# Two of chunk 1's tiles get their output projection inside the last group's steps, the other six tiles form one pipeline, and the FFN takes chunk 1 first

## The reference

```python
x = x + _L0_attn_ref(_layernorm(x), Wq, bq, Wk, bk, Wv, bv, Wo, bo)   # o @ Wo + bo
x = x + _L0_ffn_ref(_layernorm(x), ...)    # (silu(x Wg) * (x Wu)) Wd, 704 hidden, int weights
x = x + _L1_attn_ref(_layernorm(x), Wq, Wk, Wv, Wo)
x = x + _L1_ffn_ref(_layernorm(x), ...)    # 768 hidden, float8 weights with scales
```

## Time and profile before

| what | value |
|---|---|
| time, median of 3 runs | 446.37 us (446.0 to 446.38) |
| the profiled execution: time, span | 448.61 us, 446.9 us |
| PE busy | 414.6 us (93%) |
| DVE, ACT, POOL busy | 300.9, 235.1, 161.0 us |
| output projection, layer 0: first "on" to first FFN matmul | 165.05 to 180.77 us |
| the same, layer 1 | 388.37 to 405.89 us |

### The profile page before, as it was taken

One profiled execution on the slowest core, in us unless ns is written; L12 is line 12 of the kernel. 1 busy time (PEld: TensorE's weight loads), 2 busy tenths in 40 slices (PEclk: granted clock), 3 DMA queues, 4 the chain that ended last, 5 costly groups with the idle time before them and its releaser, 6 DMA issues.

```text
span 446.9 us, 14541 instructions
## 1 busy us (share of the span) xinstructions
PE 414.6 (93%) x6328; PEld 237.3 (53%) x6328; DVE 300.9 (67%) x608; ACT 235.1 (53%) x381; POOL 161.0 (36%) x242
## 2 busy tenths in 40 slices
PE   5799989999999979999999998998999999797997
PEld 5356654455555338444476465644545553384476
DVE  4635699999997118421335568899999971188883
ACT  3635545677677872311101552465776778725950
POOL 4118323202202232296881000235362553321780
PEclk9989999999999999999999998899999999999999
DMA  6799550000000000201000476400000000000002
GB/s 201 119 249 277 108 146 4 4 3 4 4 3 4 4 7 1 72 1 67 5 0 0 129 201 180 133 4 4 4 2 4 4 5 2 2 1 0 2 23 72
DMA packets 21657, 22.97 MB, mean 51 GB/s; under 512 B 2588, under 2 KB 20858, under 8 KB 21594
## 3 DMA queue, kind: packets, MB, share of 16 engines
q1 hardware_dynamic: 20498, 19.03, 17.0%
q0 software_dynamic: 544, 2.49, 1.8%
q10 hardware_dynamic: 552, 0.53, 0.4%
HBM read 8.27 MB, written 1.05 MB: 21 GB/s over the span
## 4 chain that ended last, share of the span: by engine, by line
PE 69%; DVE 17%; ACT 5%; DMA 3%; issue 3%; SPq 2%; POOL 1%; ACTq 0%; DVEq 0%
PE ps L701 11%; PE ps L721 11%; DVE mx L1110 11%; PE ps L679 10%; PE ps L803 8%; PE ps L868 5%; PE ps L808 5%; ACT prob L997 4%; PE ps L825 4%; PE ps L836 4%; PE ps L616 3%; DMA col_rows<-in_L_ffn_up_scale 3%; PE ps L687 2%; DVE stats L1074 1%; DVE xn L1183 1%
## 5 line engine op out<-in xcount | busy, mean ns | idle before, releaser
L1110 DVE TENSOR_REDUCE mx<-ps 128x1 f32<-128x512 f32 (+3 forms) x304 | 182.1, 654 | 25.7 <-PE ps L687 23.1
L997 ACT ACTIVATE prob<-ps 128x1024 f32<-128x1024 f32 (+1 forms) x192 | 145.5, 812 | 70.4 <-PE ps L701 69.8
L679 PE MATMUL ps<-kS,qS 99*32 99x512 bf16 (+18 forms) x1536 | 114.2, 322 | 5.1 <-DVE mx L1110 2.7
L530 POOL TENSOR_SCALAR_AFFINE_SELECT prob<-prob 128x256 f32<-128x256 f32 x128 | 51.9, 412 | 161.0 <-ACT prob L997 159.7
L701 PE MATMUL ps<-qS,kS 101*32 101x512 bf16 (+7 forms) x1536 | 96.6, 329 | 4.0 <-ACT prob L997 3.7
L721 PE MATMUL ps<-prob,v 128*32 128x512 f32 (+3 forms) x768 | 80.1, 489 | 2.1 <-POOL prob L530 1.4
L679 PEld LDWEIGHTS ps<-kS,qS 99*32 99x32 bf16 (+1 forms) x1536 | 43.8, 96 | 53.1 <-DVE mx L1110 29.1
L701 PEld LDWEIGHTS ps<-qS,kS 101*32 101x32 bf16 (+1 forms) x1536 | 35.3, 96 | 32.6 <-ACT prob L997 16.8
L684 PE MATMUL ps<-mask_q,identb 128*32 128x32 bf16 (+1 forms) x1024 | 52.2, 186 | 0.0
L687 PE MATMUL ps<-mask_q,identb 128*32 128x64 bf16 (+1 forms) x512 | 45.9, 198 | 0.0
L803 PE MATMUL ps<-xnT,gu0T 128*128 128x512 f32 x80 | 34.8, 594 | 0.7 <-ACT xnT L907 0.7
(11 more groups left out here) (141 smaller groups left out, 551.0 us busy)
## 6 DMA issues: line engine op xcount, KB each, us to landing
qS<-parts SPq DMA_DIRECT2D x24, 128.0 KB, 3.1
kS<-parts SPq DMA_DIRECT2D x24, 128.0 KB, 3.0
qS<-prob SPq DMA_DIRECT2D x12, 128.0 KB, 7.1
kS<-prob SPq DMA_DIRECT2D x12, 128.0 KB, 6.6
qS<-xn SPq DMA_DIRECT2D x12, 128.0 KB
kS<-xn SPq DMA_DIRECT2D x12, 128.0 KB, 2.6
out<-x SPq DMA_DIRECT2D x8, 128.0 KB, 1.7
oT<-in_L_ffn_gate_w POOLq DMA_DIRECT2D x1, 768.0 KB
```

The source lines that it names most:

```text
L530: nc.gpsimd.affine_select(out=square, in_=square, compare_op=ALU.is_ge, fill=0.0, base=0, pattern=[[0, 2], [1, P]], channel_multiplier=-1) ...
L679: mmi = nc.tensor.matmul(span[r:r + STRIP, 0:seen], qS[0:K_MAX[L], c, g * G + h, qt * P + r:qt * P + r + STRIP], kS[0:K_MAX[L], g * G + h, ...
L997: nc.scalar.activation(prob[:, n % 3, 2 * pair:2 * pair + 2, off:CH], ps[:, 2 * (m % 2):2 * (m % 2) + 2, off:CH], ACT.Exp, scale=SCALE).th ...
L1110: ins = nc.vector.tensor_reduce(mx[:, slot, qt, heads[0]:heads[-1] + 1, part], src, AX_X, ALU.max)
```

## The change

Chunk 1's tiles 4 and 5 (`EARLY`) get their three jobs inside the last pair's steps. `E_STEPS` places them: (1, 1) means step s1, behind its second scores; place 2 is behind the product with `v`. They use banks 4 to 6, with semaphores of their own, `e_full` (PE) and `e_free` (DVE). For them DVE, not ACT, copies `onT`.

The six other tiles form one pipeline in the order `RING`. At its last iteration with an "on" job, PE also transposes chunk 1's four normalised tiles. POOL, not DVE, normalises these (`xn_pool`). The FFN takes chunk 1 first; chunk 0's transposes stand behind 2 (layer 0) or 3 (layer 1) hidden tiles (`TURNS_BEHIND`), and DVE normalises chunk 0 behind its first FFN product. ACT's Silu table is loaded behind the ring's first `onT` copy. `FIRST_HALF_AFTER` becomes 6, with layer 0's "down" in the order 4, 5, 0, 1, 2, 3, 6, 7.

```diff
+FFN_C = (1, 0)
+TURNS_BEHIND = (2, 3)
+DOWN_ORDER = ((4, 5, 0, 1, 2, 3, 6, 7), (4, 5, 6, 7, 0, 1, 2, 3))
+LN_PAIRS = ((0, 1, 2, 3), (2, 3, 0, 1), (2, 0, 1, 3), (2, 3, 0, 1))
+EARLY = (4, 5)
+RING = (6, 7, 0, 1, 2, 3)
+E_STEPS = {(1, 1): [("on", 4)], (2, 0): [("turn", 4)], (2, 1): [("on", 5)], (2, 2): [("wo", 4)],
+           (3, 0): [("turn", 5)], (3, 2): [("wo", 5)]}
-FIRST_HALF_AFTER = 5
+FIRST_HALF_AFTER = 6
...
+                    if n // 2 % 2 and first >= TPC:
+                        pool.wait_ge(rstd_done, pair + 1)
+                        for t in (first, first + 1):
+                            nc.gpsimd.tensor_scalar(xn[:, t], x[:, t], mv[:, t, 0:1], rstd[:, t:t + 1],
+                                                    ALU.subtract, ALU.mult).then_inc(xn_pool, 1)
...
+            def early_job(L, kind, t):
+                bank = ps[:, e_bank(L, kind)]
+                if t > TPC:
+                    e_left(pe, L, kind, t - 1)
+                if kind == "on":
+                    if t == TPC:
+                        pe.wait_ge(m_free, (L + 1) * N_MAX)
+                        pe.wait_ge(o_taken, (L + 1) * N_CG - 1)
+                    mmi = query_major(bank, t)
+                elif kind == "turn":
+                    e_left(pe, L, "on", t)
+                    mmi = dim_major(bank, t)
+                else:
+                    e_left(pe, L, "turn", t)
+                    mmi = times_wo(L, bank, t)
+                mmi.then_inc(e_full, 1)
...
+                    if n == len(RING) - 1:
+                        ln_transposes("ffnT", 2 * L + 1, FFN_C[0], L, *((take_a, a_full) if L == 0 else (take_b, b_full)))
...
+                for kind, t in E_JOBS:
+                    dve.wait_ge(e_full, e_made(L, kind, t))
+                    bank = ps[:, e_bank(L, kind)]
+                    if kind == "on":
+                        divide(bank, t).then_inc(e_free, 1)
+                    elif kind == "turn":
+                        nc.vector.tensor_copy(onT[:, t % 2].rearrange("p j q -> p (j q)"), bank[:, 0:C]).then_inc(e_free, 1)
+                    else:
+                        nc.vector.tensor_tensor(x[:, t], bank[:, 0:C], x[:, t], ALU.add).then_inc(e_free, 1)
+                        e_left(dve, L, kind, t)
+                        ln_stats(t)
```

More of the change, by code:

```diff
@@ L205, in pace, with early @@
         return int(here)
+    last = len(exp_steps()) - TPC
+    def early(s, place):
+        order.extend(("early",) + job for job in E_STEPS.get((s - last, place), []))
     at = 0.0
@@ L215, in attention_order @@
             order.append(("pv", s - PV_LAG))
+        early(s, 2)
         at += wide(s)
@@ L535, in rstd_of @@
                 for pair in range(2 * n, 2 * n + 2):
-                    tiles = slice(2 * (pair % 4), 2 * (pair % 4) + 2)
+                    first = 2 * LN_PAIRS[n // 2][pair % 4]
+                    tiles = slice(first, first + 2)
                     pool.wait_ge(stats_done, pair + 1)
@@ new lines, in times_wo @@
+            def times_wo(L, bank, t):
+                for j in range(CJ):
+                    mmi = nc.tensor.matmul(bank[:, 0:C], onT[:, t % 2, j], attn_w(L, 3)[:, j, :], start=j == 0, stop=j == CJ - 1)
+                return mmi
+            def early_job(L, kind, t):
[14 more added lines that the diff above has]
+                mmi.then_inc(e_full, 1)
@@ L1002, in _ @@
                     take_o(s)
-                nc.scalar.activation(warm[:], nhalf[:, 0:1], ACT.Silu)
-                for t in range(NT):
-                    bank = bank_a(("onT", L, t))
-                    if t >= 2:
-                        act.wait_ge(b_full, B_AT["wo", L, t - 2] + 1)
-                    nc.scalar.copy(onT[:, t % 2].rearrange("p j q -> p (j q)"), bank[:, 0:C]).then_inc(a_free, 1)
                 def transposed_half(half):
```

236 lines of the change are left out of this document (144 added, 92 removed).

## The result

The changed kernel takes **442.94 us** (median of 6 runs, 441.25 to 443.93). The kernel before, in the runs made beside it, takes 446.22 (6 runs, 444.95 to 448.36). The measured ratio is 0.9905, with a 95% interval of 0.9875 to 0.9934; it isn't the quotient of the two medians, which is 0.9926 and lies in the interval too. It is faster, by about 3.3 us going by the medians. The prediction said 442.2 us, with a range of 440.4 to 444.8. A few executions ran at a visibly lower granted clock throughout (540.39 us at 0.753 in one case); the ratios leave them out.

A forecast was written before the change was run, and what follows sets the result against it. PE bounds the kernel, busy 93%; winnable was the stretch from the last attention step to the first FFN matmul (15.72 and 17.52 us). 1.7 + 2.9 - 0.4 = 4.2 us off 446.37 gives 442.2, range 440.4 to 444.8.

The forecast's parts named there:

- Part 1: Attention's tail: the early jobs, at isolated prices, make the ring start 2.6 us late, with two tiles done.
- rival 1: Early jobs in the attention's tail cost cheaper stream prices, 0.65 us a layer less: 440.9 or 439.9 us; chance 0.15.
- The drain between modes: Attention's tail: twelve added tiling-mode changes a layer drain PE; with the drain 442.2 us, without it 440.9.
- rival 3: No change: six early jobs in the tail cost 0.33 us more each, 2.0 us a layer: 446.2 us; chance 0.09.
- Part 2: Silu table load between the ring's first and second onT copies: about 0.3 us lost, ends nothing or 1.1.
- Part 3: Ring's end, fewer tiles, overlapped transposes, POOL 0.55 us a tile: FFN earlier by 1.7 (layer 0), 2.9 us (layer 1).
- rival 4: POOL's normalising of tiles 6 and 7 becomes the bound; gain gone at 1.84 us a tile, slower beyond; chance 0.06.
- POOL's room: Layer 1's pipeline end: POOL has 0.6 us to spare before its normalising delays the FFN.
- Part 4: Inside the FFN: layer 0 loses nothing, layer 1 loses 0.4 us at chunk 0's transposes, ends 0 and 1.4.

The follow-up runs named there:

- POOL twice: Against the changed kernel, POOL normalises each of chunk 1's tiles two times, the second time for real; 451.91 us, ratio 1.0106.
- variants but the last: The last variant is "POOL twice" with three unused PE multiplications added to fill PE's wait for tile 6; 449.50 us, ratio 1.0084.

## Why the prediction was right, and where it was off

The time and the sign came out, but the gain is put together otherwise than forecast, and one term was off by more than a factor of two.

- **Part 1, the start of the ring: right, with a little luck.** "wo" of tile 5 was forecast 7.2 us behind the copy (166.2 - 158.99) and came at 7.30, the first "turn" at 10.2 and came at 10.29. PE was ready for that "wo" 0.34 us earlier, at 6.96, 0.2 less than reckoned; DVE's copy behind tile 4's statistics, which the prediction called covered by a hair, held it. The two misses cancel in part. The isolated prices nearly carried over; rival 1's 0.65 us a layer isn't there. The prediction put the delay at 2.6 us against 3.22 for two tiles, without saying that a ring that starts with tile 4 would need no early jobs for the rest of the gain; that comparison shows their own worth, 0.07 us.
- **The drain between modes: small.** The Trainium skill, TensorEngine Tiling (Array Packing), section Key Properties, says that a change of mode drains the engine. The runs agree: two changes fewer gave 0.28 us a layer. The size of rival 3 (0.33 us more a job) isn't there.
- **Part 2, the table: right in kind, 0.3 forecast.** The prediction's own terms (2.64 and 0.1 to 0.2 against 2.58) give 0.16 to 0.26 and were rounded up. It delayed the loop by 0.17 us, and taking it out of the ring gave 0.12 and 0.08.
- **Part 3, POOL's tile: the step that failed.** "I take 0.55", from a row with one factor per partition, with 0.90 as the far end. The operation has two such factors, another pair of operations and an fp32 input, and takes 1.22 us. Put into the prediction's own formula of rival 4 (the FFN at 177.8 + 2p and at 401.1 + 2p), p = 1.22 gives distances of 21.25 and 21.23 us; measured are 21.32 and 21.28. The mechanism of that rival was right, only its price is short of the 1.84 at which the change loses; "POOL twice" goes past it and loses. The gain in layer 0 was forecast at 1.7 and is 0.46 us; in layer 1 at 2.9 and is 2.30, as POOL's room there was used up and passed. (The prediction says 0.6 us of room; its own formula gives 403.0 - 402.2 = 0.8 at 0.55 us a tile.)
- **Where layer 1's gain comes from.** The prediction reckoned it as one chain and did not name a part that measured 0.69 us: DVE's block of normalising disappears from the stretch in which DVE is the last to be waited for. By the runs, the 2.30 us are 0.40 from the ring, 0.69 that layer 1 has more without any overlap, and 1.21 from the overlap. That the 0.69 is DVE's block is read from two traces, where the additions come 0.72 us sooner behind PE; no run put the block back.
- **Part 4: right for layer 0 and the end of its "down"; too dear for layer 1.** Its FFN takes 22.15 us up to "down" where it took 22.05 (427.94 - 405.89); the gap at the second transposes is 0.34 us where 0.7 was forecast, so 0.1 and not 0.4 is lost.
- **The sum.** 0.46 + 2.30 - 0.10 = 2.66 us, where the prediction had 4.2. The medians differ by 3.28 us (interval 2.9 to 5.6), so the hit of the forecast is partly luck: some 0.6 us of it lie outside the distances, where nothing in the diff explains a gain. All variants but the last show such a surplus of their time over their distances, of 0.5 to 1.5 us.
- **Where the surplus lies: in the granted clock.** Each execution has a mean granted clock, and it comes in steps of 0.003 to 0.004. That is what one stretch of 3.4 us at half clock makes of some 440 us, and it costs up to 1.7 us. At 0.991 and 0.992 the kernel before takes 446.2 us (median of 33 executions), at 0.996 it takes 444.9 (4 executions), at 0.987 to 0.989 447.5 (19). The changed kernel has 442.92 and 443.93 us at 0.992 and four times 441.25 to 442.98, median 442.3, at 0.995 and 0.996. Compared at equal clock the gap is 2.8 and 2.6 us, from few executions, and agrees with the 2.66 of the distances. For the changed kernel and the nine variants without a second pass together (66 executions at 0.991 or above), the surplus over the distances has a median of 0.2 us at equal clock. The rest of the 3.28 is thus that the kernel before more often has one such stretch more: 24 of its 61 executions are at 0.989 or below, against 5 of 71 for those ten kernels. Whether the change makes these stretches rarer or chance does is open; the two that vary in the traces, behind the start-up wait and in layer 1's attention, are both outside the rewritten stages.

## What to carry to other kernels

Work moved into another engine's shadow is worth what the engine that ends last gives back: six PE jobs in the attention's tail, with a single visible wait of 0.34 us, brought 0.07 us, since the ring behind them began 3.43 us later. When an operation is handed to a new engine, its price is the first thing to measure, in its exact form (pair of operations, per-partition factors, types), because a neighbouring row was off by 2.2 times and moved the bound to that engine. Whole times hide such things in the scatter of the start-up and of the clock; a distance between two events around the change, read in each profile, resolves 0.1 us, and times compare best between executions of equal mean granted clock.
